# State-space layer: the skip term D·x enters the sums by a diagonal matmul, and VectorE multiplies by the gate

## What is computed

```python
xs = silu(causal_conv(x_part) + conv_b)          # 256 channels
dt = softplus(x_dt @ W_dt.T + b_dt)
dA, dBx = exp(dt * A), dt * B * xs               # 16 states for each channel
h = dA_t * h + dBx_t                             # along the sequence
y = sum_n(h * C) + xs * D
return (y * silu(z)) @ W_out.T
```

## Time and profile before

| | us |
|---|---|
| median of 3 runs | 1555.7 |
| the three runs | 1547.37, 1555.7, 1558.65 |
| profiled execution, its time | 1560.02 |
| profiled execution, its span | 1558.2 |

### The profile page before, as it was taken

The page is one execution under the profiler, slowest core; times in us unless marked ns, Lnnn a source line. Parts: engine busy times, 40 slices in busy tenths (PEclk is TensorE's granted clock), DMA queues, the critical chain, the costliest instruction groups (busy, mean ns, idle before and its releaser), DMA issues. The chain is left out here.

```text
span 1558.2 us, 31374 instructions
## 1 busy us (share of the span) xinstructions
PE 1203.3 (77%) x11216; PEld 931.3 (60%) x11216; DVE 1029.1 (66%) x2332; ACT 910.8 (58%) x1721; POOL 814.5 (52%) x654
## 2 busy tenths in 40 slices
PE   6779879889777588888539994599975999837992
PEld 2556666666666356666539993266652666626992
DVE  2999999999999656887511113477644799742444
ACT  3778868878875167776225554277743766513443
POOL 1987887887785421556645552211002246674662
PEclk9899999999999678988569997699996999957996
DMA  5203203202200230011157775300004001127885
GB/s 185 89 28 111 83 28 110 84 28 110 83 28 1 58 56 8 29 33 35 43 177 231 223 231 169 88 9 15 16 18 114 9 26 36 44 78 206 251 244 179
DMA packets 98158, 140.10 MB, mean 90 GB/s; under 512 B 13709, under 2 KB 77242, under 8 KB 93716
## 3 DMA queue, kind: packets, MB, share of 16 engines
q1 hardware_dynamic: 86708, 120.41, 25.5%
q0 software_dynamic: 9088, 17.07, 3.2%
q10 hardware_dynamic: 2208, 0.61, 0.2%
HBM read 107.52 MB, written 28.16 MB: 87 GB/s over the span
## 5 line engine op out<-in xcount | busy, mean ns | idle before, releaser
L318 POOL TENSOR_TENSOR M_dbx<-M_u,M_b_sb 128x1024 f32<-128x1024 f32 x128 | 300.0, 2363 | 57.9 <-DVE M_h L377 57.2
L377 DVE TENSOR_TENSOR_SCAN M_h<-M_pA,M_dbx 128x512 f32<-128x512 f32 x256 | 297.4, 1200 | 5.9 <-POOL M_dbx L318 5.0
L530 ACT ACTIVATE M_pA<-M_dt,M_a_neg 128x504 f32<-128x504 f32 x256 | 174.7, 683 | 51.6 <-DVE M_h L377 47.0
L540 ACT ACTIVATE M_hc<-M_pT,M_cT 128x256 f32<-128x256 f32 x256 | 119.3, 467 | 55.1 <-PE M_pT L670 53.0
L2368 PE MATMUL X_bank<-F_xT,F_wbuf 128*128 128x256 f32 x624 | 150.4, 385 | 0.0
L670 PE MATMUL M_pT<-M_ident,M_h 128*128 128x128 f32 x512 | 83.6, 288 | 81.0 <-ACT M_hc L540 45.6
L2019 POOL DMA_INDIRECT F_slots<-F_line,F_pos x128 | 127.2, 993 | 36.0 <-issue 36.0
L686 PE MATMUL M_pY<-M_ident,M_hc 128*128 128x128 f32 x1024 | 141.0, 283 | 0.0
L670 PEld LDWEIGHTS M_pT<-M_ident,M_h 128*128 128x128 f32 x512 | 58.3, 145 | 133.2 <-DVE M_h L377 70.7
L686 PEld LDWEIGHTS M_pY<-M_ident,M_hc 128*128 128x128 f32 x1024 | 131.7, 200 | 1.2
L1615 ACT ACTIVATE X_pt_sb<-X_bank 128x512 f32<-128x512 f32 x128 | 76.4, 597 | 93.0 <-PE X_bank L1747 93.0
(11 more groups left out here) (329 smaller groups left out, 2786.3 us busy)
## 6 DMA issues: line engine op xcount, KB each, us to landing
M_b_sb<-M_rows_bc SPq DMA_DIRECT2D x32, 1024.0 KB, 4.7
F_wbuf<-in_F_wcat SPq DMA_DIRECT2D x39, 578.0 KB, 3.9
F_wbuf<-in_F_wcat SPq DMA_DIRECT2D x39, 450.0 KB, 4.0
X_s_sb<-F_slots SPq DMA_DIRECT2D x39, 132.0 KB, 3.8
F_xblk<-F_slots SPq DMA_DIRECT2D x39, 132.0 KB, 3.9
F_line<-F_line SPq DMA_DIRECT2D x16, 256.0 KB, 2.7
X_kT<-F_answers SPq DMA_DIRECT2D x8, 512.0 KB, 5.6
X_kv<-in_ctxT SPq DMA_DIRECT2D x2, 1344.0 KB, 10.1
```

What stands on the lines that cost most here:

```text
L318: pool.tensor_tensor(dbx[:, k % DBXS, :, :], u[:, g % 2, :, :], bc(b_sb[:, n, :], 1, 2), ALU.mult).then_inc(dbx_ready, 1)
L377: v.tensor_tensor_scan(h[:, k % STATES, half, :], pA[:, (2 * k + half) % DECAYS, :, :].rearrange("p b t -> p (b t)"), dbx[:, k % DBXS, hal ...
L530: act.activation(pA[:, (2 * k + half) % DECAYS, :, 1:SEQ], dt[:, g % 2, half, :].rearrange("p (b t) -> p b t", t=SEQ)[:, :, 1:SEQ], ACT.Ex ...
L540: act.activation(hc[:, k % SCALED, t, :], pT[:, 0, t, :], ACT.Identity, scale=cT[:, g % 2, t, n:n + 1]).then_inc(hc_ready, 1)
```

## The change

1. A new SBUF tile d_diag holds two 128 x 128 matrices, identity times D, one for each half of the channels. VectorE builds it at the start with two tensor_scalar instructions.
2. `add_state` at n = 0 gets two more matmuls, d_diag times xs of the first 256 tokens, for both halves, into pY.
3. `turn_sum` opens its bank with a zero matmul, adds d_diag times xs of the last 256 tokens in the same way, and turns the sums back by fp32 matmuls with the identity as the moving operand, which accumulate, in place of transposes, which do not.
4. VectorE's skip_first and skip_last become gate_first and gate_last: the operation is now a product of the PSUM sums and z.
5. GpSimd's gate is gone, and its semaphore y_ready; those who waited for it wait for y_used, which VectorE raises after gate_last.

```diff
@@ gpsimd
-            def gate(g):
-                pool.wait_ge(y_used, g + 1)
-                pool.wait_ge(zg_ready, g + 1)
-                pool.tensor_tensor(y_sum[:, :, :], y_sum[:, :, :], z[:, g % 2, :, :], ALU.mult).then_inc(y_ready, 1)
...
-                if n == 8 and c >= 1:
-                    gate(c - 1)
...
-            gate(GROUPS - 1)
@@ vector
-            def skip_first(g):
+            def gate_first(g):
                 v.wait_ge(y_psum, (g + 1) * N)
+                v.wait_ge(zg_ready, g + 1)
                 reach(v, o_psum, g)
                 for half in range(2):
-                    ins = v.scalar_tensor_tensor(y_sum[:, half, 0:HALF], xs[:, g % 3, half, 0:HALF],
-                                                 d_skip[:, half:half + 1], pY[:, half, :], ALU.mult, ALU.add)
+                    ins = v.tensor_tensor(y_sum[:, half, 0:HALF], pY[:, half, :], z[:, g % 2, half, 0:HALF], ALU.mult)
                 ins.then_inc(ya_used, 1)
 
-            def skip_last(g):
+            def gate_last(g):
                 v.wait_ge(yb_psum, g + 1)
                 for half in range(2):
-                    ins = v.scalar_tensor_tensor(y_sum[:, half, HALF:GROUP], xs[:, g % 3, half, HALF:GROUP],
-                                                 d_skip[:, half:half + 1],
-                                                 bank("yB", g)[:, half * HALF:(half + 1) * HALF], ALU.mult, ALU.add)
+                    ins = v.tensor_tensor(y_sum[:, half, HALF:GROUP], bank("yB", g)[:, half * HALF:(half + 1) * HALF],
+                                          z[:, g % 2, half, HALF:GROUP], ALU.mult)
                 ins.then_inc(y_used, 1)
...
+            for half in range(2):
+                ins = v.tensor_scalar(d_diag[:, half, :], ident[:, :], d_skip[:, half:half + 1], None, ALU.mult)
+            ins.then_inc(diag_ready, 1)
             layer_norm(1)
@@ scalar
             def copy_z(g, half):
-                reach(act, y_ready, g - 1)
+                reach(act, y_used, g - 1)
@@ tensor, add_state
                     if g == 0:
                         pe.wait_ge(c_ready, 1)
+                        pe.wait_ge(diag_ready, 1)
                     pe.matmul(pY[:, :, :].rearrange("p a b -> p (a b)"), zeros[:, 0:P], zeros[:, :], start=True,
                               stop=False)
+                    for half in range(2):
+                        pe.matmul(pY[:, half, :], d_diag[:, half, :], xs[:, g % 3, half, 0:HALF], start=False, stop=False)
@@ tensor, turn_sum
+                pe.matmul(bank("yB", g), zeros[:, 0:P], zeros[:, :], start=True, stop=False)
+                for half in range(2):
+                    pe.matmul(bank("yB", g)[:, half * HALF:(half + 1) * HALF], d_diag[:, half, :],
+                              xs[:, g % 3, half, HALF:GROUP], start=False, stop=False)
                 for t in range(2):
                     for half in range(2):
-                        ins = pe.transpose(bank("yB", g)[:, half * HALF + t * P:half * HALF + (t + 1) * P],
-                                           acc[:, g % 2, t, half * P:(half + 1) * P], ident[:, :])
+                        ins = pe.matmul(bank("yB", g)[:, half * HALF + t * P:half * HALF + (t + 1) * P],
+                                        acc[:, g % 2, t, half * P:(half + 1) * P], ident[:, :],
+                                        start=False, stop=(t == 1 and half == 1))
                 ins.then_inc(yb_psum, 1)
@@ tensor, project_out
-                    pe.wait_ge(y_ready, g + 1)
+                    pe.wait_ge(y_used, g + 1)
```

More of the change, by code:

```diff
@@ L198, in mamba_phase @@
         zeros = m.sb("zeros", [P, GROUP], BF16)
+        d_diag = m.sb("d_diag", [P, 2, P])
         conv_w = acc[:, :, :, :].rearrange("p a b t -> p (a b t)")
@@ L220, in mamba_phase @@
         y_psum, ya_used, yb_psum, y_used = m.sem("y_psum"), m.sem("ya_used"), m.sem("yb_psum"), m.sem("y_used")
-        y_ready, o_psum, o_done = m.sem("y_ready"), m.sem("o_psum"), m.sem("o_done")
+        diag_ready, o_psum, o_done = m.sem("diag_ready"), m.sem("o_psum"), m.sem("o_done")
         block = ctx.enter_context(nc.Block())
@@ L437, in _ @@
                 if n == 2 and c >= 1:
-                    skip_first(c - 1)
+                    gate_first(c - 1)
                 if k < K:
@@ L444, in _ @@
                 if n == 4 and c >= 1:
-                    skip_last(c - 1)
+                    gate_last(c - 1)
                 if n == 12 and c >= 1:
@@ L454, in _ @@
                         make_dt(c + 1)
-            skip_first(GROUPS - 1)
-            skip_last(GROUPS - 1)
+            gate_first(GROUPS - 1)
+            gate_last(GROUPS - 1)
             residual(GROUPS - 1)
```

## The result

The changed kernel takes 1566.84 us (median of 5 runs, 1566.11 to 1569.39) against 1555.7 us before (median of 5): ratio 1.0068, 95% interval 1.0041 to 1.0094. It is slower by 0.7%, inside the stated range and within the 1% that was called no change. The profiled execution took 1566.11 us, its span is 1564.3; before, 1560.02 and 1558.2.

The account below looks back on a forecast made before the run. VectorE was taken as full, with TensorE the path from its restart to VectorE's wait at n = 3. Sum: 0.2 + 7 x (0.85 + 0.70) = 11.1, less 0.5, less 3.1: +7.5 us, giving 1563 us (+0.5%), range 1552 to 1574.

Parts of the forecast that it names:

- What bounds: Changed layer: VectorE is full and waits for TensorE, 11.8 us; 2.35 us taken from GpSimd per group gives nothing back.
- add_state: the failed term: Two added matmuls at n = 0 lengthen VectorE's wait at n = 3 by 0.85 us in groups 1 to 6.
- the other bound of 1.7: Upper cost in us of add_state's two matmuls if all run at the low clock and the rise comes later by as much.
- grows by over 1.5 us: Sign in the trace after: VectorE's wait at n = 3 growing this much means the forecast is wrong through the clock.
- the clock stays low longer: Rival, 14%: added matmuls cost 1.7 and turn_sum 1.52 us a group; 22.5 less 3.6 gives +19 us, 1575.
- turn_sum: TensorE's step 3: +1.52 us less 0.82 slack, so VectorE waits 0.70 us more at n = 4, groups 1 to 7.
- Group 0: First group of the layer: 0.68 us of slack before VectorE comes, so add_state's matmuls cost only +0.2 us.
- n = 11: No wait was forecast at this step; TensorE's lateness was to end at n = 5, with over 2 us of room.
- The gates: VectorE's gate pairs 0.05 to 0.10 us shorter than 0.86; only gate_last counts, 7 x 0.07 = -0.5 us.
- The end of the layer: After the last group: project_out starts 1.3 us earlier, full clock saves another 1.8; together -3.1 us, bounds -1.3 and -3.1.
- d_diag, the new wait, y_used: Building d_diag, about 0.5 us, hides before a 5.85 us load wait; zg_ready's silu is done earlier, y_used comes earlier: nothing.
- VectorE's port: Rival, 6%: lighter GpSimd frees the shared port for L361, 2.90 us falling to 1.2; 11.9 us back, 1551.

Follow-up runs that it names:

- e3: Only the first half of each group gets the diagonal matmul and VectorE gate, the last half as before the change; ratio to before 1.0067, next block starts at 519.1 us.
- e2: The changed kernel plus 16 useless zero matmuls in TensorE's idle time of step n = 1 in every group; ratio to before 0.9943, next block starts at 511.4 us.
- e5: The kernel before plus 15 useless zero matmuls in TensorE's idle time of step n = 1; next block starts at 504.0 us, ratio 0.9926 on another chip.
- e4: Only the last half of each group gets the new turn_sum and VectorE gate, the first half as before the change; ratio 0.9986, next block starts at 518.2 us.
- e1: The changed kernel with both halves' diagonal matmuls moved into TensorE's idle time of step n = 1; ratio to before 0.9931, next block starts at 509.0 us.
- e12: The changed kernel with diagonal matmuls and nine extra zero matmuls in TensorE's idle time at n = 1; ratio to before 0.9917, next block starts at 501.6 us.
- e10: The kernel before, unchanged, third trace, on the chip of the second; next block starts at 513.2 us and takes 91.7 us to its first F_stats.
- e9: The kernel before, unchanged, second trace; next block starts at 513.3 us and takes 87.0 us to its first F_stats.

## Why the prediction was right or wrong

The time lies in the range, and slower by less than 1% is what was forecast as likeliest. The working behind it was right in where the cost comes in and wrong in one term, the clock behind add_state. The layer came out at +15.8 us instead of +7.5, and the total came near by luck: the blocks that the sum took as unchanged ran 9.7 us shorter in the profile.

- *What bounds.* Right: VectorE is full, and the cost came in as its waits for TensorE at n = 3 and n = 4. GpSimd's waits for the scans rose from 57.2 to 89.5 us; the time taken from it was given to waiting.
- *add_state: the failed term.* "The end of the chain moves by 0.85 us if the clock rises at the same moment." The condition did not hold. The columns cost about their 0.85 (groups 3 and 5 of e3), but in most groups the low stretch doubled from 3.4 to 6.8 us and the wait grew by 1.96 (group 4), past the other bound of 1.7 too. By the prediction's own sign (the wait "grows by over 1.5 us") the forecast is wrong here, and the rival "the clock stays low longer", with 14%, is what happened in the layer. Its 1.7 + 1.52 = 3.22 us a group are near the 3.16 measured, but made of other terms (1.96 at n = 3, 0.62 at n = 4, the rest in smaller delays), and its sum for the layer, 22.5 less 3.6, was too much against 15.8, since groups 1 and 7 paid less. e2 against e5 shows the forecast's sum where the gap is filled: 7.4 us for 7.5, with VectorE's waits 12.6 - 2.8 = 9.8 us longer where 7 x 1.55 = 10.9 were put.
- *turn_sum.* +0.70 at n = 4 forecast, 0.62 measured in each of groups 1 to 7, and 0.61 to 0.62 in e4.
- *Group 0.* 0.2 forecast; VectorE's step n = 3 comes 0.41 us later.
- *n = 11.* The forecast had the lateness end at n = 5. A wait of 0.36 us comes at n = 11 in groups 1 to 5, behind project_out at the low clock.
- *The gates.* A pair takes 0.75 instead of 0.86 us; 0.05 to 0.10 was the bound, 0.11 is the result.
- *The end of the layer.* -3.1 forecast. From the start of L700's weights to that of the residual it was 512.01 - 503.75 = 8.26 us; from L696's weights it is 527.80 - 522.63 = 5.17: -3.1. The clock stayed up, as argued. The two rows of before:

```profile
503.75 0.47 PEld L700 LDWEIGHTS M_pM<-M_ident,M_acc 128*128 128x128 f32 x4
...
512.01 0.69 DVE L416 TENSOR_TENSOR L_x<-M_pM,L_x 128x512 f32<-128x512 f32 x1 [6.29 <-PE M_pM L712]
```

- *d_diag, the new wait, y_used.* No cost to be seen; no run tested them alone.
- *VectorE's port.* The rival has fallen: rounding_of_1p takes 2.90 us after the change too. Once, before the loop starts, it runs while GpSimd is idle, and takes 1.22:

```profile
32.56 1.22 DVE L354 SCALAR_TENSOR_TENSOR M_e<-M_e1p,M_e 128x1024 f32<-128x1024 f32 x1 [12.14 <-ACT M_e1p L516]
...
319.05 2.90 DVE L354 SCALAR_TENSOR_TENSOR M_e<-M_e1p,M_e 128x1024 f32<-128x1024 f32 x1
```

- *The rest of the kernel.* The sum took it as unchanged. It was 9.7 us shorter in the profile. The three traces of before alone differ by 11.8 us in span with layers that end within 0.6 us of each other, so a forecast of a few us for a layer cannot be read off the whole time; it has to be read at the layer's end. Measured there, +7.5 should have been +13.5 to +16.4, by which of the traces are compared.

The corrected sum for the layer: 0.4 in group 0; in group 1 +0.8 at n = 3; in groups 2 to 6 some +3.1 each; in group 7 less; together the 18.3 us by which step n = 3 of group 7 is later (481.33 against 463.06), + 0.6 at its n = 4, - 3.1 at the end = 15.8.

## What to carry to other kernels

Before adding work to an in-order queue, look for where that queue is idle: here the same change made the layer 15.8 us longer with its matmuls ahead of a wait, and 4.8 us shorter with them one or two steps earlier. Where TensorE's clock falls around an idle time, added work may not be paid by its columns alone: the two parts cost 5.3 and 4.4 us alone and 13.5 to 15.8 together. A few useless matmuls in the gap are then the cheapest experiment, run on both kernels, so that the clock's part of the change can be told from the rest. And judge a change to one stage at the end of that stage: later stages can give or take as much as the change itself.

## What the runs showed of the hardware

- Where the clock fell around TensorE's restart in groups 1 to 7 of the layer, it stayed low for 3.4 or 6.8 us. In group 4 of the kernel before it fell 0.3 us before the restart and the stretch was 3.4 us; in group 4 of the changed kernel it fell 1.6 us before the restart and the stretch was 6.8; in e1, 0.3 us behind it, and 3.4.
- After 2.64 us of idle time the clock fell in e1; in group 4 of e12, with nine zero matmuls ahead of the diagonal ones and 0.91 us left idle, it did not.
- The fp32 records of 256 columns follow each other by 0.215 us at the high level (L698) and 0.43 at the low (L681), those of 128 columns by 0.112 (L686) and 0.21 (L715, eight from 327.02 to 328.73).
- In the next block the clock stayed at 0.50 for 20.3 us with TensorE 92% busy (e10), in the same place where it was 1.00 in e9 with TensorE 79% busy. The Trainium skill (TensorE: Matmul & The Clock Gate, Part 1) describes the clock as one that is released by sustained activity and throttled without it. The layer agrees with that, in that the clock fell around idle time in before and stayed up in groups 1 to 6 of e2, where that time was filled; the stretch in e10 does not fit it, and why is open.
- A VectorE tensor_tensor of PSUM and one SBUF tile was not held up by GpSimd's running instruction (gate pairs of 0.74 to 0.76 us throughout), also where GpSimd's dbx ran all through them (306.34 in group 4, beside L314 from 305.07 to 307.43). An instruction with two SBUF operands (L354) took 2.89 or 2.90 us in the seven groups of the loop and 1.22 at 32.56, with GpSimd idle.
